# Quantised codes written as low bytes of preset 16-bit words, and the weight split on VectorE alone, in a three-layer block

## The reference, cut to what matters

```python
# layer 1: fake-quantised matmul against a context of 1024 rows per sequence
q = clip(round(v / scale + zp), 0, 255); fake(v) = (q - zp) * scale
x = x + matmul(fake(layernorm(x)), fake(ctx))        # ctx: (16, 1024, 1024)
# layer 2: causal attention with 32 heads of 32, rotary positions
qkv = layernorm(x) @ qkv_w + qkv_b
x = x + softmax(rope(q) @ rope(k).T / sqrt(32) + mask) @ v @ out_w + out_b
# layer 3: one dense layer with a low-rank update
x = x + layernorm(x) @ W.T + bias + lora(layernorm(x))
```

## Time and profile before

| | us |
|---|---|
| median of 3 runs | 742.89 (742.68 to 744.18) |
| the profiled execution's own time | 746.89 |
| its span, first to last instruction | 745.1 |
| PE busy, share of span | 677.3, 91% |
| DVE busy | 552.3, 74% |
| ACT busy | 331.1, 44% |
| POOL busy | 76.7, 10% |
| DVE's code passes (L706), 100 of them | 72.2 |
| ACT's code passes (L322), 28 of them | 29.2 |

### The profile page before, as it was taken

The page is one execution under the profiler, slowest core; times in us unless marked ns, Lnnn a source line. Parts: engine busy times, 40 slices in busy tenths (PEclk is TensorE's granted clock), DMA queues, the critical chain, the costliest instruction groups (busy, mean ns, idle before and its releaser), DMA issues.

```text
span 745.1 us, 13305 instructions
## 1 busy us (share of the span) xinstructions
PE 677.3 (91%) x4784; PEld 343.9 (46%) x4784; DVE 552.3 (74%) x1090; ACT 331.1 (44%) x395; POOL 76.7 (10%) x57
## 2 busy tenths in 40 slices
PE   1656977999999999999999999999999999999998
PEld 0122434544544554455445544644554455454553
DVE  7899987648866876887599658767874477877761
ACT  6976676234832663374438334823660033210100
POOL 1156240020001001000200020001001000000000
PEclk9867988899999999999999999999999999999999
DMA  9998465163525543363535163524552043022321
GB/s 351 408 327 304 164 217 172 42 217 117 179 70 183 161 149 113 113 193 116 169 116 194 57 225 117 188 80 150 182 180 88 1 145 139 29 85 71 113 70 57
DMA packets 35160, 112.72 MB, mean 151 GB/s; under 512 B 4536, under 2 KB 4664, under 8 KB 35136
## 3 DMA queue, kind: packets, MB, share of 16 engines
q1 hardware_dynamic: 32288, 103.83, 40.9%
q0 software_dynamic: 2560, 8.43, 3.0%
q10 hardware_dynamic: 288, 0.13, 0.1%
HBM read 99.78 MB, written 8.39 MB: 145 GB/s over the span
## 4 chain that ended last, share of the span: by engine, by line
PE 32%; DVE 28%; issue 22%; DMA 7%; ACT 6%; POOL 2%; DVEq 0%; POOLq 0%; SPq 0%; ACTq 0%
PE dense L997 7%; PE dense L999 6%; PE dense L998 6%; ACT code L315 4%; PE cross L1128 4%; DMA raw<-in_ctx 4%; PE turn L987 3%; DVE wq_l L273 3%; DMA xa<-in_x 3%; PE dense L1095 3%; DVE xa L714 3%; DVE smx L741 2%; DVE at L738 2%; POOL xb L606 2%; DVE code L706 2%
## 5 line engine op out<-in xcount | busy, mean ns | idle before, releaser
L997 PE MATMUL dense<-wq_h,xn_h 128*128 128x512 f16 x448 | 174.5, 389 | 9.6 <-DVE wq_l L273 9.6
L999 PE MATMUL dense<-wq_h,xn_l 128*128 128x512 f16 x448 | 173.6, 387 | 0.0
L315 ACT ACTIVATE code<-raw,cst,qc 128x1024 uint8<-128x1024 f32 x112 | 136.9, 1235 | 75.3 <-DMA raw<-in_ctx 60.6
L998 PE MATMUL dense<-wq_l,xn_h 128*128 128x512 f16 x384 | 149.5, 389 | 0.0
L706 DVE TENSOR_SCALAR code<-code 128x1024 f16<-128x1024 uint8 x100 | 72.2, 759 | 23.3 <-ACT code L315 22.9
L1021 PE MATMUL cross<-code,q1t 128*128 128x512 f16 x256 | 73.4, 400 | 13.8 <-DVE q1t L694 5.3
L997 PEld LDWEIGHTS dense<-wq_h,xn_h 128*128 128x128 f16 x448 | 44.2, 99 | 70.8 <-issue 14.7
L999 PEld LDWEIGHTS dense<-wq_h,xn_l 128*128 128x128 f16 x448 | 44.7, 100 | 55.4 <-issue 4.4
L725 DVE TENSOR_TENSOR rope<-dense,cst 128x512 f32<-128x512 f32 x32 | 22.0, 688 | 59.5 <-PE dense L999 59.1
L998 PEld LDWEIGHTS dense<-wq_l,xn_h 128*128 128x128 f16 x384 | 38.2, 100 | 37.8 <-issue 2.8
L997 PE MATMUL dense<-wo_h,rope 128*128 128x512 f16 x128 | 48.8, 381 | 1.1 <-DVE rope L758 1.1
(11 more groups left out here) (120 smaller groups left out, 1052.1 us busy)
## 6 DMA issues: line engine op xcount, KB each, us to landing
raw<-in_ctx SPq DMA_DIRECT2D x112, 512.0 KB, 3.7
wo_h<-in_ctx SPq DMA_DIRECT2D x8, 512.0 KB, 9.5
at<-in_qkv_w SPq DMA_DIRECT2D x8, 512.0 KB, 9.1
wo_l<-in_ctx SPq DMA_DIRECT2D x8, 512.0 KB, 8.8
wo_h<-in_qkv_w SPq DMA_DIRECT2D x8, 512.0 KB, 8.3
wo_l<-in_qkv_w SPq DMA_DIRECT2D x8, 512.0 KB, 9.1
at<-at SPq DMA_DIRECT2D x32, 128.0 KB, 2.4
x_scratch<-xb POOLq DMA_DIRECT2D x8, 512.0 KB, 6.3
```

The lines of the kernel that those rows point to most:

```text
L315: act.activation(code8[:, c % U8, :], src, ACT.Identity, scale=qc[:, 1:2], bias=z2).then_inc(s_u8, 1)
L997: pe.matmul(bank[:, :], a_h[:, k, :], w_hi, start=(n == 0 and not started), stop=False)
L998: pe.matmul(bank[:, :], a_h[:, k, :], w_lo, start=False, stop=False)
L999: ins = pe.matmul(bank[:, :], a_l[:, k, :], w_hi, start=False, stop=(n == KC - 1))
```

## The change

Nine edits, in one:

1. `code8` and `code16` become one float16 ring `code` of 6 slots. DVE fills it once with words of value 1024 (0x6400). `quantise` writes its uint8 results into the low byte of every word (step of 2 bytes), so that a word reads 1024 + code. `codes`, `act_codes` and their semaphores go. The residual's correction takes 1024 in place of 128.
2. `quantise` of chunk c now waits for PE to have used the slot: chunks 6 to 15 for chunk c-6 of the same pair, 0 to 3 for 12 to 15 of the pair before, 4 and 5 for 10 and 11 of it. PE's `chunk` waits for `quantise` directly.
3. All 32 low parts are made on DVE; POOL's and ACT's scaling pass go.
4. Pair 0's raw chunks get 16 places of their own: eight in the out projection's weights, eight in k's. The q tiles are staged where v's weights will stand, the k tiles in the out projection's, v's in `at` and the out projection's, and the out tiles one place ahead of where they end: tile 25's high part overwrites the staged tile 24, and so on. A staged tile is then two pieces of 2 KB in each partition.
5. The transfers' order: q's tiles 2 and 3 move from behind chunk 15 to behind chunk 9, and the rest as in the diff.
6. In `pair`, ACT's and DVE's order of tiles changes; `q(3)` moves behind `qk_evac(0)`.
7. The blocks of `qkv` run q, q, k, k, v, v instead of q, k, q, k, v, v, so that the first two need q's tiles alone.
8. A Newton step takes two instructions in place of three.
9. DVE clears 128x3072 float32 (the ring) before its other first instructions.

```diff
+CODE_BASE = 1024.0
+RAW, RING = 2, 6
-        code8 = sb("code8", [P, U8, DM], U8T)
-        code16 = sb("code16", [P, QR, DM], F16)
+        code = sb("code", [P, RING, DM], F16)
+        o_stage = [wo[:, :, n, :].bitcast(F32) for n in range(KC)]
+        k_stage = [wq[:, :, n, DM:2 * DM].bitcast(F32) for n in range(KC)]
+        v_stage = [wq[:, :, n, 2 * DM:3 * DM].bitcast(F32) for n in range(KC)]
+        def slot_before(c):
+            return c - RING if c >= RING else max(k for k in range(CHUNKS) if code_slot(k) == c) - CHUNKS
...
         def staged(j):
+            if j < KC:
+                return v_stage[j]
+            if j < 2 * KC:
+                return o_stage[j - KC]
+            if j < 2 * KC + 4:
+                return at_stage[:, j - 2 * KC, :, :]
+            if j < W_QKV:
+                return o_stage[j - 2 * KC - 4]
+            return o_stage[j - W_QKV + 1] if j < W_ALL - 1 else lnt_stage
...
             def weight_hi(j):
+                act.wait_ge(s_w[j], 16)
+                if 2 * KC <= j < W_QKV:
+                    act.wait_ge(s_wlo, j - 2 * KC + 1)
                 if j == W_QKV:
+                    act.wait_ge(s_wlo, 2 * KC + 5)
+                elif j > W_QKV:
+                    act.wait_ge(s_wlo, j)
+                act.activation(weight_parts(j)[0], staged(j), ACT.Copy, scale=WSC).then_inc(s_whi, 1)
             def quantise(i, c):
...
+                if above(CHUNKS * i + slot_before(c) + 1):
+                    act.wait_ge(s_cmm, CHUNKS * i + slot_before(c) + 1)
+                low_bytes = code[:, code_slot(c), :].bitcast(U8T).rearrange("p (a n b) -> p a n b", a=2, b=2)[:, :, :, 0]
+                act.activation(low_bytes, src, ACT.Identity, scale=qc[:, 1:2], bias=z2).then_inc(s_u8, 1)
```

ACT's order in `pair` (its old lines left out):

```diff
+                w(*range(8, 19))
+                q(0, 1)
+                w(19, 20)
+                q(2)
                 qk_evac(i, 0)
+                w(21)
+                q(3)
+                w(22)
                 q(4)
+                w(23)
                 q(5)
                 qk_evac(i, 1)
                 a_high(i + 1, 0)
                 a_high(i + 1, 1)
+                q(6, 7, 8, 9)
                 qk_evac(i, 2)
                 qk_evac(i, 3)
+                w(24)
+                q(10)
+                w(25)
+                q(11)
                 v_evac(i, 0)
                 exponent(i, 0)
+                w(26)
                 exponent(i, 1)
+                w(27)
                 q(12)
                 v_evac(i, 1)
                 p_evac(i, 0)
+                w(28)
                 q(13)
```

SP, the end of its list for pair 0:

```diff
+            for j in range(24, 30):
+                load_weight(j)
+                load_chunk(1, j - 14)
+                if j == 27:
+                    v_swap(0, 0)
+                    v_swap(0, 1)
```

DVE, `mean_rstd`:

```diff
                 for n in range(3):
-                    link(dve.scalar_tensor_tensor(t, y, v, y, ALU.mult, ALU.mult))
-                    link(dve.tensor_scalar(t, t, -0.5, 1.5, ALU.mult, ALU.add))
-                    link(dve.scalar_tensor_tensor(y, y, scale if n == 2 else 1.0, t, ALU.mult, ALU.mult))
+                    link(dve.tensor_scalar(t, h, y, y, ALU.mult, ALU.mult))
+                    link(dve.scalar_tensor_tensor(y, t, 1.5, y, ALU.subtract, ALU.mult))
```

DVE's order in `pair` (old lines left out):

```diff
+                w(4, 8)
                 rotate(i, 0)
+                w(8, 11)
                 rotate(i, 1)
+                w(11, 16)
                 norm1(i + 1)
                 rotate(i, 2)
                 a_low(i + 1, 0)
                 a_low(i + 1, 1)
+                w(16, 20)
                 rotate(i, 3)
+                w(20, 24)
                 cross_evac(i + 1, 0)
                 softmax_in(i, 0)
                 softmax_in(i, 1)
+                w(24, 26)
                 softmax_out(i, 0)
+                w(26, 27)
                 softmax_out(i, 1)
+                w(27, 28)
```

PE, `pair`:

```diff
                 qkv(i, 0, due=tiles_due(0) if weights else None)
-                qkv(i, 1, due=tiles_due(KC) if weights else None)
+                qkv(i, 1)
                 qk_turn(i, 0, ahead)
-                qkv(i, 2)
+                qkv(i, 2, due=tiles_due(KC) if weights else None)
```

## The result

The changed kernel takes 761.6 us (median of 4, 758.28 to 763.88) beside 743.03 of the kernel before in the same session: a ratio of 1.0244, with a 95% interval of 1.0204 to 1.0283. It is slower by 2.4%. I had forecast 742.7 in a range of 735 to 749, and even the slower rivals stopped at 747.7.

A forecast was written before the change was run, and what follows sets the result against it. It took PE to bound the loop pairs and layer 3, and DVE's chain pair 0. From the median of 742.9, pair 0's -3.5 and the loop's +3.3 gave 742.7 us, in a whole range of 735 to 749.

The forecast's parts named there:

- A loop pair: Pairs 1 to 6: quantise 6 waits for chunk 0, scores make PE wait 2.0; net +0.55 a pair, +3.3 in all.
- the term of pair 0: Pair 0 with its start: scores 8.2 us earlier, 4.9 given back at the out tiles, -0.2: -3.5, open by 4.
- Rival 2: Loop pairs: PE gains nothing at `qkv(4)`, so scores come later; +1.35 a pair, 747.5 us; chance 0.22.
- Rival 1: Loop pairs: the evacuations are in time, so scores come earlier; 737.3 us, or 731.9 at the extreme; chance 0.32.
- Newton's steps: Each LayerNorm: one of three linked instructions dropped per step, about 0.5 us less; hidden in layer 3 and pair 7.
- The start: Before pair 0: 1.7 - 0.5 + 1.2, so pair 0 starts 2.4 us later, at 47.3.
- The order term: At the start: q's tiles 2 and 3 go before c15, so `cross_evac` begins 1.7 us later.
- Pieces of 2 KB cost nothing: Start's transfers: W's load in 2 KB pieces ran at 407 GB/s, 4 KB ones at 409, so no cost.
- The port's +1.2: Before pair 0: POOL's bias add beside `norm2(0)` slows DVE's small instructions; +1.2 us, between 0 and 1.8.
- Rival 4: Before pair 0: POOL's add keeps the shared ports, DVE stands up to 2.0 us, not 1.2; 743.5 us; chance 0.03.
- Rival 3: Pair 0 gives nothing: alternating out tiles, half clock and byte writes 0.3 longer eat its 3.5 and 1.5 more; 747.7 us; chance 0.12.
- Byte writes of ScalarE: ACT's quantising: single-byte writes with a step of 2 cost 0 over the packed bytes' 1.235 us; double at most.

The follow-up runs named there:

- experiment 6's first kernel: Kernel before with only its eight first-stage buffers made pairs of 2 KB halves, so chunks and weight tiles arrive in 2 KB pieces: 741.27 us, ratio 1.0003.
- experiment 4: Changed kernel, but from pair 1's codes on chunks 6 and 7 are written as packed bytes into `pt` without waiting, then converted by VectorE: 735.55 us, ratio 0.9892.

## Why the prediction was wrong

*"A loop pair ... Net +0.75 ... six times: +3.3."* This step failed, and it carries the larger part of the miss: the loop took 13.1 more and not 3.3, 9.8 of the 17.4 by which the whole was off between the two profiled runs. The other 7.6 are in the term of pair 0, below. Each link of the loop's chain held: quantise 6 2.2 later (forecast 2.3), 9.24 to the scores (9.37), waits of 1.54 to 1.95 (2.0), no wait before the fifth block. The idle time it adds up to was +2.5. What the sum did not have is that TensorE runs slower after such a wait: +10.6. I used that fact for pair 0 ("PE also falls to 1.2 GHz where it waits") and not for the loop, where the earlier trace rows show 1.00 throughout, because no wait of before was as long: its longest is 0.86.

*Rival 2, "the ring's wait at its full price"*, had the sign and the place, at 747.5. But its reason, that PE gains nothing ahead of the fifth block, did not come true, and its price was still one of idle time only. *Rival 1* is out by the waits of 1.54 to 1.95: the evacuations were not in time.

*What the change was worth without that wait* was undervalued. I gave Newton's steps only the 0.6 us before the fifth block, and took 69.5 as a pair's length. Alone they give 6 us, with pairs of 67.93. Two LayerNorms of a pair are 0.4 shorter each. Why the rest of the 1.5 goes with it is not settled; the profiled execution of before was also one of its slower ones (746.89 in a spread of 739 to 748), and experiment 6's first kernel, the same in the loop, has pairs of 68.7 to 69.1. That waits were hidden behind a bound I took as fixed is the same error as above in the other direction.

*The start, "+2.4".* It was +4.0; pair 0's term below contains it. The order term was mis-sized: +1.7 forecast, 3.7 by its own run. "Pieces of 2 KB cost nothing" rested on a stretch of 2 us with other transfers; over 10 us they run at 386 to 392 GB/s. At 388 GB/s 21 transfers of 0.524 MB take 28.4 us, not the 26.9 of 409, and in the changed kernel VectorE stands for 11.61 ahead of `cross_evac` (below), so its work does not hide it. The port's +1.2 did not come: `norm2(0)` beside POOL's pass took 3.68 (from 40.65 to the last row here). Before it took 4.08, and the difference is that of the Newton steps.

```profile
37.54 0.74 DVE L648 SCALAR_TENSOR_TENSOR xa<-cross,qc,xa 64x512 f32<-64x512 f32 x1 [11.61 <-PE cross L938]
...
40.68 0.69 DVE L591 BATCH_NORM_STATS2 st<-xa 128x6 f32<-128x512 f32 x1
40.73 2.34 POOL L552 TENSOR_TENSOR xb<-xa,outb 128x1024 f32<-128x1024 f32 x1 [18.77 <-DVE xa L649]
...
42.81 0.27 DVE L600 TENSOR_SCALAR nw<-nw 128x1 f32<-128x1 f32 x1
...
44.33 0.81 DVE L624 TENSOR_SCALAR lnt<-xa,mv,nw 128x1024 f32<-128x1024 f32 x1
```

Rival 4 is out by the same rows: POOL's pass ends at 43.07, and VectorE had gone on beside it from 40.68. The Trainium skill ("SBUF — State Buffer", section "Who interferes with whom") says that a VectorE instruction with at most one input from SBUF, outside the two-port modes, does not contend with GpSimd. Those that ran beside the pass here, the two statistics and the small ones up to 43.07, have at most one besides their per-partition scalars, and none was held up, so the trace agrees. I had applied the page's rule without that part.

*Pair 0, "-3.5".* This sum counts from the start of the run, so it says when pair 1 begins: 153.48, where it was 149.39. It was +4.1, a miss of 7.6. The scores came at 101.88, not 97.5. VectorE's chain itself was right (31.8, from 57.45 to 89.28, forecast 32), but it began 2.4 later than my 55, as q's first block ended later. Behind it chunk 6's quantising began after 2.55 us and not 1.1, and from there to the scores it took 10.05 and not 9.4:

```profile
101.88 1.39 PE L982 MATMUL score<-at 32*64 32x64 f32 x32 [2.21 <-ACT at L299]
```

From the scores to the last copy it was 35.1, forecast 31.3: the out tiles did alternate as I had followed them, but slower. For the -0.2 at the end of the sum the prediction gives no reason; from the last copy to pair 1 it was 0.7 less than before. The changed kernel's ScalarE in pair 0, chunks 6 and 7, 8, 9, and two of the out tiles:

```profile
91.83 2.37 ACT L285 ACTIVATE code<-raw,cst,qc 128x1024 uint8<-128x1024 f32 x2 [12.54 <-PE cross L938]
96.25 1.24 ACT L285 ACTIVATE code<-raw,cst,qc 128x1024 uint8<-128x1024 f32 x1 [2.05 <-PE cross L938]
99.61 1.24 ACT L285 ACTIVATE code<-raw,cst,qc 128x1024 uint8<-128x1024 f32 x1 [2.12 <-DMA raw<-in_ctx]
...
109.97 1.06 ACT L272 ACTIVATE wo<-wo 128x1024 f16<-128x1024 f32 x1 [6.08 <-DVE wo L640]
...
123.66 1.06 ACT L272 ACTIVATE wo<-wo 128x1024 f16<-128x1024 f32 x1 [4.43 <-DMA wo<-in_out_w]
```

Most of the wait of 12.54 is the length of VectorE's chain, as PE comes to chunk 0 only behind it: PE's last wait for a low part ends at 89.42. In experiment 4, where chunks 6 and 7 do not wait for PE, ScalarE still stands there for 7.04 us, as `pt` first has to be free of staged weights. Without the ring's wait the scores come at 97.39 and the pair takes 97.32, 7.3 less. Some 0.8 of that is there before the wait can act, as VectorE's chain begins at 56.69 and not 57.45. That the scores' 97.39 is so near my 97.5 is luck: mine had the ring's wait in it. From the scores to the last copy experiment 4 has 33.2, so 1.9 of the 3.8 lost there are not the ring's. Rival 3's sign for pair 0 was right; how much of the rest is half clock, which it also named, no run separates.

*Byte writes of ScalarE*: 0 as forecast, not rival 3's 0.3. From the groups of the page, 1238 ns beside the 1235 of the earlier trace rows:

```profile
L285 ACT ACTIVATE code<-raw,cst,qc 128x1024 uint8<-128x1024 f32 x112 | 136.7, 1238 | 97.3 <-DMA raw<-in_ctx 61.9
```

## What to carry to other kernels

Where TensorE is the bound and runs at its full clock, price a new wait of 1.5 us or more in a loop at about twice its length, not at its length, and look at the loop's longest wait of before. Between the changed kernel and that of experiment 4, 10.4 us of waits at the scores went with 22.7 us of loop. The price is rough: in the eleven kernels with such waits, the loop was longer than in experiment 4 by 1.2 to 2.7 times the sum of each pair's longest wait. When a buffer ring gets fewer slots than the distance at which it is filled, ask what the producer is queued with: here a filler that waits holds up a stream of loads, and with it everything behind it on the same engine. Four other orders did not cure that here; two more buffers did, even borrowed ones that cost two extra passes on an idle engine. And try the smallest part of a large change alone: the shorter Newton steps alone gave 0.9923, and the whole change, with experiment 4's edit, 0.9892.

## What the runs showed of the hardware

*The clock.* Over the 102 loop pairs of the seventeen profiled kernels, by the longest wait of PE in the pair: under 1.2 us (none lies between 0.86 and 1.25), all 36 pairs have a granted clock of 1.00; of 8 with 1.2 to 1.6 it is 5; of 16 with 1.6 to 1.8, 8; of 18 with 1.8 to 2.1, 4; of 24 with more, 2. The same wait at the same place may or may not bring it down (1.65 and 1.72 in the first two pairs shown above). A fall shows as 1.3 to 6 us more busy time in a pair. Falls came with the wait at the scores, at a transpose and ahead of a chunk alike. The Trainium skill ("TensorE: Matmul & The Clock Gate", section "HAM oscillation — how this bites in real kernels") tells of a wait that recurs in every step of a loop and brings the clock down in every step; here it recurs, and brings it down in four pairs of six, behind waits of under 2 us.

*Transfers.* Pieces of 2 KB ran at 386 to 392 GB/s over 10 us, pieces of 4 KB at 406 to 411. The 358 GB/s that the prediction cited are, by the Trainium skill ("Perfetto Trace Analysis", section "Roofline"), the share of a core whose neighbour reads too, and one core alone may pull more; the trace agrees, with 409.

*Small VectorE instructions.* The new step's `tensor_scalar` on 128x1 with two per-partition scalars takes 0.27 us, the one with constants 0.15.
